# A four-stage attention and expert kernel: order of one step of the linear attention, a query scale moved, biases split early, fewer semaphore clears

## The chip, the cores and the metric

The kernel runs on one core of a Trainium2 chip. The metric is the device time of one execution in microseconds (us); three executions of the kernel before gave 4503.48, 4504.20 and 4504.74 us (median 4504.2). "TensorE" is the matrix engine (PE in the rows, PEld for its weight loads), "VectorE" is DVE, "ScalarE" is ACT, "GpSimd" is POOL, and "SyncE" is SP, which here only starts transfers.

## The reference, cut to what matters

Two layers are computed over 4096 tokens of width 256. Only the first part of the first layer is touched:

```
def _L0_attn_ref(X, Wq, Wv, q_norm_w, v_norm_w):
    K = X.reshape(B, L, H, d)                        # 16 heads of 16
    Q = rms_norm_multihead((X @ Wq.T).reshape(B, L, H, d), q_norm_w)
    V = rms_norm_multihead((X @ Wv.T).reshape(B, L, H, d), v_norm_w)
    W = jnp.cumsum(jnp.einsum('blhd,blhe->blhde', K, V), axis=1)
    return jnp.einsum('blhd,blhde->blhe', Q, W).reshape(B, L, D)
x = x + _L0_attn_ref(_layernorm(x), ...)
x = x + _L0_ffn_ref(_layernorm(x), ...)              # router: logits, top 2 of 16 experts
x = x + _L1_attn_ref(_layernorm(x), ...)
x = x + _L1_ffn_ref(_layernorm(x), ...)              # top 8 of 64 experts
```

## The kernel before

The program has seven stages, each a block of five instruction streams, one per engine, that meet only through semaphores: `linear_attention` (names la_), `experts` (ex_), `project` (pj_), `softmax_attention` (at_), `output_projection` (op_), `expert_pairs` (ep_) and `add_odd` (ao_). After each stage, `release` (L200 to L203) lets GpSimd clear the semaphores of the stage and then makes all engines wait for each other.

The first stage handles the tokens in 32 tiles of 128. It is a software pipeline: a loop over steps i from -12 to 41 is written out on every engine, and in step i an engine works on several tiles at once. Step i of TensorE (L794 to L842) is, in this order:

- `logits(i-8)`: the router's logits of a tile normalised earlier (L699). It first waits for `xa_ready`, VectorE's add of tile i-1 to x (L466). In one step of four (i = 12, 16, ...) `positions` (L711 to L716) follows, which needs the mask that VectorE's `choose` computes at the end of its previous step (L479 to L492).
- `queries(i+2)` and `keys(i+5)`: transposes (L723, L729). The keys need `xn`, which ScalarE writes (L602) after `roots` (L646), which needs VectorE's `squares_sum` (L448).
- `project(i+4)`: the query and value projection (L739).
- `outputs_T(i)`: state times queries (L749) and the masked scores times values (L757). It needs the state, a sum that GpSimd makes (L387) behind its two multiplications L369 and L376.
- `scores(i+1)` (L769), which VectorE then masks (`masked`, L440).
- `routed(i-7)` (L776), `outputs(i)` (L782), `update(i)` (L790).

VectorE's step is: router work of the group if there is any, `masked(i+1)`, `squares_sum(i+4)`, `update(i)` (the new key-value product times a block mask, L463, and the add to x, L466), statistics, `roots`, and in one step of four `choose` or `place`. Steps 27 and later have no keys left to transpose and steps 28 and later no projection; the logits run eight tiles behind and go on to step 39.

After the last `place`, GpSimd writes the routing table with indirect transfers (`scatter`, L396, two for a tile). The biases of the experts are loaded into buffers of the pipeline once these are free (L339 to L342), split into three bf16 parts by VectorE (L512 to L520, called in step NT+2 = 34), and stored to DRAM.

## Time and profile before

| | |
|---|---|
| median of three runs | 4504.2 us |
| the profiled execution's own time | 4506.27 us |
| its span | 4504.5 us |
| linear attention, from the start to the first instruction of the expert stage | 437.07 us |
| TensorE busy, whole span | 3984.1 us (88%) |

The span is divided by the semaphore barriers into stages, so a stage is read on its own: what it saves moves everything behind it forward. In a row of a timeline the first number is the start in us, the second the time from the first start to the last end, and `xN` how many instructions were merged; in brackets at the end stands how long the engine sat idle before and who ended it.

### The profile page before, as it was taken

How to read it: one execution, taken by the hardware profiler on the slowest of the kernel's cores; microseconds unless marked ns; L12 is line 12 of the kernel's file. 1: busy time of each engine (PE TensorE's matmuls, PEld its weight loads, DVE VectorE, ACT ScalarE, POOL GpSimd, SP SyncE). 2: the span in 40 equal slices, each digit the busy share in tenths (PEclk: the TensorE clock that was granted, in tenths of full speed). 3: DMA queues.
4: the chain of work that ended last, by engine and by line, in shares of the span. 5: the costliest groups of instructions: out<-in, count | busy, mean ns of one | idle time of the engine just before them, and what ended most of it. 6: DMA issues, size and time to landing. Idle time of an engine off the chain costs nothing. (4 is left out here: it accounts for less than half of the span.)

```text
span 4504.5 us, 54711 instructions
## 1 busy us (share of the span) xinstructions
PE 3984.1 (88%) x17866; PEld 3005.5 (67%) x17866; DVE 3574.9 (79%) x4436; ACT 2646.0 (59%) x3555; POOL 2209.0 (49%) x1837
## 2 busy tenths in 40 slices
PE   6774998683999999999999999999999999989563
PEld 3443554452788888888888888888888888867421
DVE  4454443774899999999999999999999999956611
ACT  4442333331677777777777777777777777742221
POOL 1234665464455555555555555555555555530154
PEclk8776999786999999999999999999999999989776
DMA  6001333666222232223222322232223223137296
GB/s 242 20 22 39 56 61 59 221 217 185 63 53 57 49 81 50 57 49 81 53 53 49 81 55 53 57 76 56 51 58 72 56 51 64 34 113 235 74 243 165
DMA packets 349678, 384.04 MB, mean 85 GB/s; under 512 B 141532, under 2 KB 279585, under 8 KB 336851
## 3 DMA queue, kind: packets, MB, share of 16 engines
q1 hardware_dynamic: 325334, 354.22, 30.8%
q0 software_dynamic: 24064, 26.32, 3.5%
q8 instruction: 147, 2.41, 0.2%
q14 instruction: 133, 1.09, 0.1%
HBM read 232.55 MB, written 117.84 MB: 78 GB/s over the span
## 5 line engine op out<-in xcount | busy, mean ns | idle before, releaser
L1523 POOL TENSOR_TENSOR at_pl<-at_pf,at_ph 128x512 fp32r<-128x512 f32 x1024 | 1330.0, 1299 | 1343.0 <-ACT at_ph L1670 1342.7
L1669 ACT ACTIVATE at_pf<-at_ps_s 128x1024 f32<-128x1024 f32 x1024 | 1051.0, 1026 | 747.5 <-PE at_ps_s L1719 747.5
L1586 DVE TENSOR_TENSOR at_pl<-at_pf,at_ph 128x512 fp32r<-128x512 f32 x1024 | 1355.4, 1324 | 20.6 <-ACT at_ph L1670 20.6
L1568 DVE TENSOR_REDUCE at_mx<-at_ps_u 128x2 f32<-128x1024 f32 x1024 | 1250.2, 1221 | 24.5 <-PE at_ps_u L1703 24.4
L1670 ACT ACTIVATE at_ph<-at_ps_s 128x1024 fp32r<-128x1024 f32 x1024 | 1042.7, 1018 | 0.0
L1719 PE MATMUL at_ps_s<-at_q,at_k 66*128 66x512 f32 x2048 | 820.7, 401 | 0.0
L1718 PE MATMUL at_ps_s<-at_q,at_k 128*128 128x512 f32 x2048 | 812.2, 397 | 0.3 <-ACT at_ph L1670 0.3
L1735 PE MATMUL at_ps_v<-at_ph,at_vh 128*128 128x512 f32 x2048 | 810.1, 396 | 0.2 <-POOL at_pl L1523 0.2
L1737 PE MATMUL at_ps_v<-at_pl,at_vh 128*128 128x512 f32 x2048 | 809.5, 395 | 0.0
L1736 PE MATMUL at_ps_v<-at_ph,at_vl 128*128 128x512 f32 x2048 | 809.2, 395 | 0.0
L1703 PE MATMUL at_ps_u<-at_k,at_qp 128*128 128x512 f32 x2048 | 648.0, 398 | 63.5 <-DMA at_q<-at_low 47.7
L1703 PEld LDWEIGHTS at_ps_u<-at_k,at_qp 128*128 128x128 f32 x2048 | 387.3, 190 | 163.6 <-issue 48.1
L1719 PEld LDWEIGHTS at_ps_s<-at_q,at_k 66*128 66x128 f32 x2048 | 387.6, 189 | 96.3
L1735 PEld LDWEIGHTS at_ps_v<-at_ph,at_vh 128*128 128x128 f32 x2048 | 389.3, 190 | 90.6 <-POOL at_pl L1523 0.6
L1736 PEld LDWEIGHTS at_ps_v<-at_ph,at_vl 128*128 128x128 f32 x2048 | 386.5, 189 | 94.6
L1737 PEld LDWEIGHTS at_ps_v<-at_pl,at_vh 128*128 128x128 f32 x2048 | 386.0, 188 | 89.9
L1718 PEld LDWEIGHTS at_ps_s<-at_q,at_k 128*128 128x128 f32 x2048 | 389.3, 190 | 84.3 <-ACT at_ph L1670 1.0
L440 DVE TENSOR_TENSOR la_at<-la_ps_a,C 128x512 f32<-128x512 f32 x128 | 79.5, 684 | 165.6 <-PE la_ps_a L769 165.6
L1191 DVE TENSOR_TENSOR pj_t<-pj_ps_e,pj_rope 128x1024 f32<-128x1024 f32 x128 | 149.7, 1216 | 62.4 <-PE pj_ps_e L1319 34.8
L1561 DVE TENSOR_TENSOR at_low<-at_raw,at_cut 128x512 fp32r<-128x512 f32 x128 | 170.0, 1328 | 18.0 <-DMA at_q<-at_low 17.9
L945 PE MATMUL ex_ps_g<-wgu,ex_xgT 128*128 x320 | 162.3, 630 | 0.0
L1661 ACT ACTIVATE at_qp<-at_q 128x512 fp32r<-128x512 f32 x128 | 143.5, 1123 | 29.6 <-DMA at_k<-kT 29.6
(254 smaller groups left out, 4116.1 us busy)
## 6 DMA issues: line engine op xcount, KB each, us to landing
at_k<-kT SPq DMA_DIRECT2D x64, 512.0 KB, 10.0
at_q<-qT SPq DMA_DIRECT2D x64, 512.0 KB, 9.3
wgu<-Wgu_in SPq DMA_DIRECT2D x64, 384.0 KB, 5.2
qT<-pj_rot SPq DMA_DIRECT2D x32, 512.0 KB, 3.1
vT<-pj_vo SPq DMA_DIRECT2D x32, 512.0 KB, 4.4
kT<-pj_rot SPq DMA_DIRECT2D x32, 512.0 KB, 3.1
at_raw<-qT SPq DMA_DIRECT2D x32, 512.0 KB, 4.7
at_raw<-kT SPq DMA_DIRECT2D x32, 512.0 KB, 6.6
```

Of the source, the lines that this page charges most:

```text
L1523: pool.tensor_tensor(pl[:, n % NP, at], pf[:, n % NP, at], ph[:, n % NP, at].bitcast(F32), ALU.subtract).then_inc(s["pl2_ready"], 1)
L1561: dve.tensor_tensor(low[:, i % 2], raw[hh][:, i * QB:(i + 1) * QB].bitcast(F32), cut[:, i % 2].bitcast(F32), ALU.subtract).then_inc(s["low ...
L1568: dve.tensor_reduce(mx[:, qb % 2, 2 * i:2 * i + 2], ps_u[:], X, ALU.max).then_inc(s["u_max"], 1)
L1586: dve.tensor_tensor(pl[:, n % NP, at], pf[:, n % NP, at], ph[:, n % NP, at].bitcast(F32), ALU.subtract)\
L1669: act.activation(pf[:, n % NP], ps_s[:, n % 2], ACT.Exp, scale=DH ** -0.5)
L1670: act.activation(ph[:, n % NP], ps_s[:, n % 2], ACT.Exp, scale=DH ** -0.5)\
L1703: m = pe.matmul(ps_u[:, w], tile, k1[hh][:, kb * QB:(kb + 1) * QB], start=True, stop=True)
L1718: pe.matmul(out, k1[hh][:, ks], q1[hh][:, qs], start=True, stop=False)
L1719: m = pe.matmul(out, k2[hh][0:MROW + 2, ks], q2[hh][0:MROW + 2, qs], start=False, stop=True)
L1735: pe.matmul(out, vh[:, hh, c], ph[:, n % NP, keys], start=c == 0, stop=False)
L1736: pe.matmul(out, vl[:, hh, c], ph[:, n % NP, keys], start=False, stop=False)
L1737: m = pe.matmul(out, vh[:, hh, c], pl[:, n % NP, keys], start=False, stop=c == KC - 1)
```

## The change

Six edits, all but the last in `linear_attention`.

1. TensorE's step begins with `queries`, `keys` and `project`; `logits` and `positions` stand between `outputs_T` and `scores`.
2. VectorE does `update(i)` ahead of `squares_sum(i+4)`.
3. The weight of the query norm is no longer applied by ScalarE to the queries (two ACTIVATEs with a scale) but by VectorE to the block mask (`blocksw`, once), by which the key-value product is multiplied. ScalarE copies the queries in one ACTIVATE.
4. The biases are loaded at the start, split in step -7 and stored then. ScalarE's first `squares` and VectorE's first `masked` wait for that.
5. The last four routed tiles alternate between two places in PSUM, with other waits.
6. The semaphores of three stages are cleared together after `project`, those of the other four at the end.

```
+            self.project()
+            self.release()
...
+            self.add_odd()
+            self.release()
...
-        def release():
-            nc.clear_and_free_semaphores(held)
-            nc.all_engine_barrier()
-        ctx.callback(release)
...
+                sp.dma_start(bsrc[:, 0:2 * F0], ins["bgu"]).then_inc(s["biases"], 16)
+                sp.dma_start(bsrc[:, 2 * F0:], ins["bd"]).then_inc(s["biases"], 16)
                 for q in range(1, Q):
                     load_x(q)
...
+                sp.wait_ge(s["bias_split"], 5)
+                sp.dma_start(self.bias_dram[:].rearrange("k e n -> e k n"), bpart).then_inc(s["bias_out"], 16)
...
-                        dve.tensor_tensor(dst, ps_k[:, 1], blocks.unsqueeze(1).broadcast_to([P, DC, P]), ALU.mult)\
+                        dve.tensor_tensor(dst, ps_k[:, 1], blocksw[:], ALU.mult)\
...
+                        link(dve.tensor_tensor(blocksw[:], blocks.unsqueeze(1).broadcast_to([P, DC, P]),
+                                               normw[:, :, 0:1].broadcast_to([P, DC, P]), ALU.mult))
+                    if i == -7:
+                        split_biases()
+                    if i == -1:
+                        dve.wait_ge(s["bias_out"], 16)
                     if tile(i + 1):
                         masked(i + 1)
+                    if tile(i):
+                        update(i)
                     if tile(i + 4):
                         squares_sum(i + 4)
                     if tile(i):
-                        update(i)
                         measure(i, (s["xa_ready"], i + 1), mv2, s["mv2_ready"])
...
-                    if i == NT + 2:
-                        split_biases()
...
-                        m = act.activation(qf[:, t % 3, c], src, ACT.Copy, scale=normw[:, c, 0:1])
-                    m.then_inc(s["q_ready"], 1)
+                    act.activation(qf[:, t % 3], ps_t[:, 1].rearrange("p (c l) -> p c l", c=DC), ACT.Copy).then_inc(s["q_ready"], 1)
...
-                    if tile(j):
-                        ...
-                        logits(j)
-                    if tile(j - 1) and (j - 1) % 4 == 3:
-                        ...
-                        positions((j - 1) // 4)
                     if tile(i + 2) or tile(i + 5):
...
                     if tile(i):
                         outputs_T(i)
+                    if tile(j):
+                        ...
+                        logits(j)
+                    if tile(j - 1) and (j - 1) % 4 == 3:
+                        ...
+                        positions((j - 1) // 4)
                     if tile(i + 1):
                         scores(i + 1)
```

TensorE in step 16, where positions come, before (la_wg is the router's weight, la_mask the mask of `choose`, la_qn and la_xn the normalised queries and tokens):

```order
L699 MATMUL la_ps_o<-la_wg,la_xrT 128x16 [waits la_xrT_ready,la_lg_ready,la_xa_ready]
L699 MATMUL la_ps_o<-la_wg,la_xrT 128x16
L711 MATMUL la_ps_o<-la_mask,tri 128x64 [waits la_mask_ready,la_seen_ready,la_lg_ready,la_xa_ready]
L713 MATMUL la_ps_o<-la_mask,ones_bf 128x48
L713 MATMUL la_ps_o<-la_mask,ones_bf 128x32
L713 MATMUL la_ps_o<-la_mask,ones_bf 128x16
L716 MATMUL la_ps_o<-la_seen,ones_bf 128x64
L723 MATMUL la_ps_t<-C,la_qn 128x128 [waits la_q_ready,la_qn_ready,la_xnT_ready,la_xrT_ready]
L723 MATMUL la_ps_t<-C,la_qn 128x128
L729 MATMUL la_ps_t<-C,la_xn 128x128 [waits la_xn_ready]
L729 MATMUL la_ps_t<-C,la_xn 128x128
L739 MATMUL la_ps_qv<-la_wqv,la_xnT 128x512 [waits la_qc_ready,la_xnT_ready]
```

and in the changed kernel the same step (its line numbers are larger by 10):

```order
L733 MATMUL la_ps_t<-C,la_qn 128x128 [waits la_q_ready,la_qn_ready,la_xnT_ready,la_xrT_ready]
L733 MATMUL la_ps_t<-C,la_qn 128x128
L739 MATMUL la_ps_t<-C,la_xn 128x128 [waits la_xn_ready]
L739 MATMUL la_ps_t<-C,la_xn 128x128
L749 MATMUL la_ps_qv<-la_wqv,la_xnT 128x512 [waits la_qc_ready,la_xnT_ready]
L749 MATMUL la_ps_qv<-la_wqv,la_xnT 128x512
L767 MATMUL la_ps_k<-la_at,la_vn 32x128 [waits la_vn_ready,la_at_ready,la_kvm_ready]
L767 MATMUL la_ps_k<-la_at,la_vn 32x128 x15
L709 MATMUL la_ps_o<-la_wg,la_xrT 128x16 [waits la_xrT_ready,la_lg_ready,la_xa_ready]
L709 MATMUL la_ps_o<-la_wg,la_xrT 128x16
L721 MATMUL la_ps_o<-la_mask,tri 128x64 [waits la_mask_ready,la_seen_ready,la_lg_ready,la_xa_ready]
```

The two waits on VectorE (`xa_ready` and `mask_ready`) no longer stand ahead of the transposes and the projection; the only wait on the way to these is now `xn_ready`.

VectorE late in the stage, step 34, before (16x768 are the biases, la_lg the logits of the seventh group):

```order
L433 SCALAR_TENSOR_TENSOR la_nb<-la_mv,la_rstd 128x4 [waits la_rstd2_ready]
L516 CAST la_at<-la_xnT 16x768 [waits la_oT_ready,la_biases]
L517 TENSOR_TENSOR la_sq<-la_xnT,la_at 16x768 [waits la_bias_split]
L518 CAST la_at<-la_sq 16x768 [waits la_bias_split]
L519 TENSOR_TENSOR la_xnT<-la_sq,la_at 16x768 [waits la_bias_split]
L520 CAST la_at<-la_xnT 16x768 [waits la_bias_split]
L472 TENSOR_TENSOR la_lg<-la_ps_o,la_bg 128x64 [waits la_l_ready,la_bias_split]
```

and VectorE at the start of the changed kernel, behind the statistics of the first tiles:

```order
L537 TENSOR_TENSOR la_pq<-C,la_normw 128x4 [waits la_norms]
L539 TENSOR_TENSOR la_blocksw<-C,la_normw 128x256
L430 BN_STATS la_stats<-x_sb 128x6 [waits la_mv1_ready,la_x1,la_own]
L431 BN_AGGR la_mv<-la_stats 128x2 [waits la_own]
L520 CAST la_at<-la_at 16x768 [waits la_biases]
L521 TENSOR_TENSOR la_sq<-la_at 16x768 [waits la_bias_split]
L522 CAST la_at<-la_sq 16x768 [waits la_bias_split]
L523 TENSOR_TENSOR la_at<-la_sq,la_at 16x768 [waits la_bias_split]
L524 CAST la_at<-la_at 16x768 [waits la_bias_split]
```

The five operations have left the place ahead of the logits of the seventh group and stand some 380 us earlier, between the statistics of the fifth and the sixth tile.

## Rows read from the trace of the kernel before

**Rows 1.** Stretches of the first stage: us, PE, PEld, DVE, ACT, POOL busy (instructions), clock, DMA share, GB/s
```profile
44.36:114.39 70.03, 49.44 (x464) 31.49 (x464) 36.42 (x90) 32.10 (x95) 12.48 (x20) 0.85 0.51 187
114.39:342.68 228.29, 163.22 (x1382) 110.05 (x1382) 113.76 (x334) 102.88 (x294) 62.38 (x83) 0.78 0.08 24
342.68:378.48 35.80, 23.29 (x272) 17.83 (x273) 20.71 (x63) 12.76 (x39) 13.20 (x16) 0.86 0.10 31
378.48:437.07 58.59, 16.52 (x115) 12.50 (x114) 28.43 (x111) 8.04 (x20) 30.52 (x29) 0.58 0.13 30
```

**Rows 2.** Who waited for whom, 44 to 380 us: total us, times, longest
```profile
DVE la_at L440 <- PE la_ps_a L769: 161.2, 31, 7.2
PE la_ps_o L699 <- DVE x_sb L466: 62.3, 23, 2.9
PE la_ps_t L729 <- ACT la_xn L602: 20.6, 7, 2.9
```

**Rows 3.** Timeline of a step without logits (63.24 to 73.46 us)
```profile
63.24 2.48 DVE L440 TENSOR_TENSOR la_at<-la_ps_a,C 128x512 f32<-128x512 f32 x4 [4.77 <-PE la_ps_a L769]
...
65.64 0.68 DVE L448 TENSOR_REDUCE la_ss<-la_sq 128x32 f32<-128x512 f32 x1
66.23 0.41 DVE L463 TENSOR_TENSOR la_kvm<-la_ps_k,C 128x256 f32<-128x256 f32 x1
...
66.56 0.42 DVE L466 TENSOR_TENSOR x_sb<-la_ps_o,x_sb 128x256 f32<-128x256 f32 x1
66.58 0.58 ACT L602 ACTIVATE la_xn<-x_sb,la_nb,la_rstd 128x256 f32<-128x256 f32 x1
...
67.22 0.69 PE L729 MATMUL la_ps_t<-C,la_xn 128*128 128x128 f32 x2 [2.94 <-ACT la_xn L602]
```

**Rows 4.** Timeline of a step with logits (126.80 to 137.65 us)
```profile
126.80 2.48 DVE L440 TENSOR_TENSOR la_at<-la_ps_a,C 128x512 f32<-128x512 f32 x4 [7.24 <-PE la_ps_a L769]
...
130.60 0.62 PE L699 MATMUL la_ps_o<-la_wg,la_xrT 128*128 128x16 f32 x4 [2.75 <-DVE x_sb L466]
...
131.53 3.35 PE L739 MATMUL la_ps_qv<-la_wqv,la_xnT 128*128 128x512 f32 x4
...
136.49 1.17 PE L769 MATMUL la_ps_a<-la_qz,la_xnT 32*128 32x256 f32 x16
```

**Rows 5.** The same windows view inside two steps, 121.6 to 128.4 us
```profile
121.60:125.00 3.40, 3.40 (x23) 2.05 (x24) 0.00 (x0) 1.61 (x5) 0.00 (x0) 0.50 0.02 5
125.00:128.40 3.40, 2.84 (x49) 2.12 (x40) 1.60 (x3) 1.01 (x3) 0.00 (x0) 1.00 0.00 0
```

**Rows 6.** Timeline of a step with positions (257.32 to 271.64 us)
```profile
264.99 0.21 PE L711 MATMUL la_ps_o<-la_mask,tri 128*128 128x64 bf16 x1 [3.17 <-DVE la_mask L492]
```

**Rows 7.** Timeline, GpSimd's state sum in step 27 (began at 342.68)
```profile
348.59 0.72 POOL L387 TENSOR_TENSOR la_state<-la_state,la_kvm 128x256 f32<-128x256 f32 x1
```

**Rows 8.** Timeline of the bias split, 394 to 402 us
```profile
394.10 1.01 PE L699 MATMUL la_ps_o<-la_wg,la_xrT 128*128 128x16 f32 x4 [0.56 <-ACT la_xrT L664]
...
397.84 0.55 DVE L516 CAST la_at<-la_xnT 16x768 bf16<-16x768 f32 x1 [7.30 <-DMA la_xnT<-bd_in]
398.42 0.95 DVE L517 TENSOR_TENSOR la_sq<-la_xnT,la_at 16x768 f32<-16x768 f32 x1
...
401.54 0.23 DVE L472 TENSOR_TENSOR la_lg<-la_ps_o,la_bg 128x64 f32<-128x64 f32 x1
```

**Rows 9.** Timeline of GpSimd alone, 398 to 408 us
```profile
398.82 1.41 POOL L396 DMA_INDIRECT table<-la_entry,la_slot  x1 [0.31 <-issue]
400.54 1.25 POOL L396 DMA_INDIRECT table<-la_entry,la_slot  x1 [0.30 <-issue]
406.65 0.98 POOL L396 DMA_INDIRECT table<-la_entry,la_slot  x1 [4.86 <-DVE la_entry L508]
```

**Rows 10.** GpSimd's release between stages, all seven: ns min/median/max, first and last start
```profile
L202 POOLq EVENT_SEMAPHORE_RANGE_CLEAR  x7: 67/240/418, 436.3 to 4504.1; - x7
```

**Rows 11.** Timeline of ScalarE at the start, 10 to 20 us
```profile
16.42 0.60 ACT L631 ACTIVATE la_sq<-la_ps_qv 128x512 f32<-128x512 f32 x1 [2.53 <-PE la_ps_qv L739]
```

More of the change, by code:

```diff
@@ L143, in __init__ @@
         self.nc, self.ins, self.out = nc, ins, out
-        self.sems = 0
+        self.held = []
     def build(self):
@@ L193, in scope, with release @@
         ps = lambda name, shape, dt=F32: ctx.enter_context(nc.psum_tensor(f"{stage}_{name}", shape, dt))
-        held = []
         def sem(name):
-            held.append(nc.alloc_semaphore(f"{stage}_{name}"))
-            return held[-1]
-        def release():
-            nc.clear_and_free_semaphores(held)
-            nc.all_engine_barrier()
-        ctx.callback(release)
+            self.held.append(nc.alloc_semaphore(f"{stage}_{name}"))
+            return self.held[-1]
         return ctx, sb, ps, sem
+    def release(self):
+        self.nc.clear_and_free_semaphores(self.held)
+        self.nc.all_engine_barrier()
+        self.held = []
     def linear_attention(self):
@@ L220, in linear_attention @@
             pq = sb("pq", [P, DC, 2])
+            blocksw = sb("blocksw", [P, DC, P])
             stats = sb("stats", [P, 2, 2, 6])
@@ L279, in linear_attention @@
             BW = 2 * F0 + D
-            bsrc, brest = (buf[0:E].rearrange("p a b -> p (a b)")[:, 0:BW] for buf in (xnT, sq))
-            bpart = at[0:E].rearrange("p h l -> p (h l)")[:, 0:3 * BW // 2].bitcast(BF16).rearrange("p (k n) -> p k n", k=3)
+            room = at[0:E].rearrange("p h l -> p (h l)")
+            bsrc, brest = room[:, 0:BW], sq[0:E].rearrange("p a b -> p (a b)")[:, 0:BW]
+            bpart = room[:, BW:BW + 3 * BW // 2].bitcast(BF16).rearrange("p (k n) -> p k n", k=3)
             below, begin = (buf.rearrange(f"p {a} -> p ({a})")[:, 0:(ST0 + 1) * E].rearrange("p (n e) -> p n e", e=E)
@@ L298, in sums, with routed_at @@
                 return (TB - 2) * (t // TB) + max(0, min(t % TB, LAST) - 1)
+            def routed_at(t):
+                return ps_qv[:, 0:D] if t >= NT - 4 and t % 2 else ps_t[:, 0]
             vn3 = vn[:].rearrange("p r g t d -> p r (g t d)")
@@ L663, in routed_T @@
                         act.wait_ge(s["l_ready"], t - 1)
[L664 removed]
+                    act.activation(xrT[:, t % 2], routed_at(t), ACT.Copy).then_inc(s["xrT_ready"], 1)
                 for i in range(FIRST, END):
@@ L823, in _ @@
                         outputs_T(i)
+                    if tile(j):
+                        if i > 0:
+                            pe.wait_ge(s["xa_ready"], min(i, NT))
+                        if j >= 4 and j % 4 == 0:
+                            pe.wait_ge(s["lg_ready"], j // 4)
+                        if j >= 5 and j % 4 == 1:
+                            pe.wait_ge(s["pos_read"], j // 4)
+                        logits(j)
+                    if tile(j - 1) and (j - 1) % 4 == 3:
+                        pe.wait_ge(s["xa_ready"], min(i, NT))
+                        pe.wait_ge(s["lg_ready"], (j - 1) // 4 + 1)
+                        positions((j - 1) // 4)
                     if tile(i + 1):
@@ L830, in _ @@
                             pe.wait_ge(s["q_ready"], i + 3)
-                        if tile(i - 8):
+                        if i - 7 >= NT - 2:
+                            pe.wait_ge(s["xrT_ready"], i - 8)
+                        elif 0 < i - 7 <= NT - 4:
                             pe.wait_ge(s["xrT_ready"], i - 7)
+                        if i - 7 == NT - 3:
+                            pe.wait_ge(s["qc_ready"], NT)
                         routed(i - 7)
```

20 lines of the change are left out of this document (3 added, 17 removed).

## Prediction

> **What bounds the kernel now.** I read the table of stages first: all but two small edits stand in linear attention, which ends at 437.07 us of 4504.5 and hands its end to the next stage through a barrier, so a microsecond saved there is one off the total. Second, the windows of that stage [rows 1]: no engine is busy throughout. From 44.36 to 342.68 us TensorE works 71% of the time at a mean granted clock of 0.85 and 0.78, VectorE 50%. Third, who waited for whom [rows 2]: VectorE's `masked` waits for TensorE's scores 31 times (161.2 us), and TensorE waits for VectorE's add to x 23 times (62.3 us, 2.7 each), in the steps without logits for `xn` instead (7 times, 20.6 us). So a step is a loop of two engines that take turns: TensorE's scores, `masked`, VectorE's chain, TensorE again. Fourth, one step of each kind. Let M be the start of `masked`. Without logits [rows 3] the tokens' statistics are at M+2.40, the key-value product at +2.99, the add at +3.33, `xn` at +3.34 and the keys at +3.98; the next M follows 6.24 us later, a step of 10.22. With logits [rows 4] these wait for the add and start at M+3.80, and the step is 10.85. Steps with positions wait once more, 3.17 us for the mask, and take 14.32 [rows 6].
>
> **The clock.** Inside a step there are stretches of some 3.4 us with the granted clock at 0.50, which is the 1.2 GHz level, and others at 1.00, the 2.4 GHz level [rows 5]; the projection runs at the lower one (3.35 us) [rows 4]. Such a stretch, in which TensorE is always busy, costs half its length, 1.70 us. The step of 10.85 had one, so it would be 9.15 without; the step of 10.22 would be 8.52. Steps 8 to 26 take 228.29 us [rows 1]; four have positions, and at 14.32 each they leave 171.0 for the other fifteen, 11.40 each. That is 2.25 above 9.15: one such stretch in every step and a second in a third of them.
>
> **The change, part by part.** All against the profiled execution, whose own time is 4506.27 us (span 4504.5 and 1.8 around it), 2.1 above the median.
>
> *Order in VectorE's step.* The product and the add now stand ahead of `squares_sum`. Their starts are 0.33 apart and the add lasts 0.42, of which some 0.07 lies beside the next operation, so `squares_sum` starts 0.68 later [rows 3]. `roots`, `xn` and the keys hang on it and come at M+4.66. In the steps with logits the add was the gate before and is no longer.
>
> *Steps 1 to 7* (70.03 us [rows 1]) have no logits; the transposes led TensorE's step already. They only lose: 0.68 each is 4.8. A longer wait before the keys may also bring a second slow stretch; in one step of five, 0.34 each, I take +1.0 a step, **+7.0**. Bounds: 0, should the later `squares_sum` be absorbed by an earlier add and statistics, and +17, if every step gets a second stretch (7 x 2.4).
>
> *Steps 8 to 26.* The new loop is: keys at M+4.66, then the 6.24 less 1.70 of a warm step without logits, 4.54, and the logits in line behind `outputs_T`, 0.62 [rows 3, 4]. That is 9.82 warm, 0.67 more than 9.15. What it gives back is the mask: positions now stand late in the step, where the mask (3.17 us behind the logits' place) has long been there, so the four steps pay only for the matmuls, about 0.4 each. The clock decides the rest. I take one slow stretch in each step and a second in one of ten, 1.87 us, since one idle stretch of TensorE per step remains and the second one, behind the logits in positions' steps, goes: 11.69 a step. 19 x 11.69 + 4 x 0.4 - 0.9 (step 16 begins a new state and has no product to wait for) = 222.8 against 228.29, **-5.5**. Bounds: with 1.70 it is 219.6, -8.7; with today's 2.25 it is 230.0, +1.7. Without the position steps there would be no gain: each of the other fifteen goes from 11.40 to 11.69.
>
> *Steps 27 to 30* (35.80 us [rows 1]). No keys are left. In step 27 the state, GpSimd's sum, is complete at M+6.63 [rows 7], and `outputs_T` can't start before it; work that stood ahead of it during that wait, the logits, now stands behind it. I take 0.62 a step, **+2.4**, bounds -1 (step 28 no longer waits for its mask) and +5 (the lower clock after the wait doubles what follows).
>
> *The biases at the end.* VectorE sat idle 7.30 us for the bias transfer and then spent 397.84 to 401.54 on five operations, while the seventh group's logits were ready at 394.10 + 1.01 = 395.11 [rows 8]. The group is ready some 6.4 us earlier. But GpSimd's scatters follow, and these are a queue: GpSimd was idle for VectorE only 4.86 us at 406.65, where 0.31 is its usual gap, so 4.55 is gained. Two scatters that lay beside the split's subtraction of 0.95 took 1.41 and 1.25 us, where the next takes 0.98 [rows 8, 9]; they should shrink by 0.43 and 0.27 as well: **-5.2**, bounds -4.55 and -6.4. [...]
>
> *The releases.* GpSimd's clear is at 436.3 and the next stage's first instruction at 437.07, 0.8 us, and there are seven [rows 1, 10]. Five go, 3.9; the semaphores that they cleared are cleared in the two that stay, about 5 x 0.24 = 1.2: **-2.7**, bounds -2.6 and -4.0.
>
> *The start.* The split now needs two transfers of 16 rows and its five operations (3.9 us as in [rows 8]) ahead of ScalarE's first `squares`. This starts at 16.42 us, after 2.53 us of waiting for the projection [rows 11], and VectorE's own work there waits for transfers of x as well; so I take **0**. If the biases land late or x by as much behind them, the whole start shifts: bound +3. The store of the split biases is waited for before tile 0's `masked`, some 20 us after the split: 0.
>
> *No term.* ScalarE copies the queries in one operation instead of two, beside a VectorE that is waited for: 0, bounds -1 and +1. The block mask product reads a tensor of the same size (0.41 us [rows 3]), one extra operation is in the start: 0. The last four routed tiles in two places: a buffer wait less at the end, 0, bound -1.
>
> Sum: 7.0 - 5.5 + 2.4 - 5.2 - 2.7 = -4.0. From 4504.2 this gives **4500.2 us**. About 9 us, 0.2%, is what a measurement of this kernel can tell from no change.
>
> **Rivals.**
>
> *A: the clock comes back.* If TensorE, opening the step with its longest piece of work and no longer stopped by the add and the mask, is granted the higher level for more of it, the mean penalty of steps 8 to 26 falls from 1.87 to, say, 1.0: 19 x 0.87 = 16.5 less, **4484**. For it: the clock is 0.86 in steps 27 to 30, where steps are short, against 0.78 [rows 1], so steps without a slow stretch exist. Against: steps 1 to 7 have this very order on TensorE, with a wait of 2.94 us for `xn` in each and a clock of only 0.85.
>
> *B: slower, by the second stretch.* The keys come 0.68 later than now in steps without logits and 0.14 later in the others, and the logits are added to the part behind them. If each step of 8 to 26 then has two slow stretches, it takes 9.82 + 3.4 less what the stretch shares with idle time, 12.7: 19 x 1.0 more, **4519**. The point from which it decides: a mean penalty above 2.16 eats the whole gain of these steps, above 2.9 the kernel is slower by 9. For it: the penalty is 2.25 now. Against: today's second stretches come with the additional stop for the mask or the add, which is gone.
>
> *C: it does not do what it says.* The mask may still be late, because `choose` also starts later, behind an update and statistics that now wait for outputs_T: then 4 x 2.5 us come back, **4510**. Against: positions moves by more than 5 us (from the step's head to behind `outputs_T`) and the wait was 3.17 [rows 6].
>
> *D: the start is bound by the biases*, +3, **4503**: inside "no change".
>
> **Chances.** Forecast with D 0.47; A 0.30, C 0.08, B 0.15. Faster by over 0.2% (under 4495.2): A and a part of the forecast's own spread (its terms at the good ends give -8.7 instead of -5.5 and +4.8 for +7.0), 0.35. Slower by over 0.2% (over 4513.2): B, 0.14. Within: 0.51. The likeliest case alone has 4492 to 4510; the range with A and most of B is 4483 to 4514.
>
> **What would show it.** Right: `masked` to keys 4.66 in every step; no wait of logits for the add or of positions for the mask; steps 1 to 7 together 75 to 79 us, steps 8 to 26 about 223 us at a clock near 0.8; the seventh group's logits on VectorE at 395 in place of 401.5 and no idle 4.86 on GpSimd; two releases. Wrong: keys at M+4.0 still in steps 1 to 7, steps 8 to 26 under 210 or over 235 us, a first `masked` later than before, or a wait in the tail that takes the place of the split.

## The result: slower by 0.2 to 0.3%, where "no change" was forecast

The changed kernel took 4516.68 us (median of 9 runs, 4512.07 to 4522.57) beside 4503.48 of the kernel before (9 runs): ratio 1.003, 95% interval 1.002 to 1.004, so 13 us slower and just above the range of 4483 to 4514. The same kernel, run once more beside the experiments, took 4508.04 us (11 runs) beside 4500.68: ratio 1.0017 (1.0008 to 1.0026), 7.4 us slower. Both say slower, the second by a time inside the range; the forecast was 4 us faster.

The profiled execution has a span of 4510.0 us, 5.5 more than before. The windows of its first stage, in the same stretches as [rows 1] (steps 1 to 7, 8 to 26, 27 to 30, and from the last `masked` to the expert stage), columns as there:

```profile
42.11:121.39 79.28, 54.05 (x464) 34.05 (x464) 35.77 (x91) 30.58 (x88) 12.49 (x20) 0.81 0.47 170
121.39:346.75 225.36, 161.01 (x1381) 105.76 (x1382) 112.50 (x333) 98.05 (x275) 62.39 (x83) 0.80 0.08 25
346.75:388.67 41.92, 29.61 (x273) 22.30 (x273) 20.62 (x64) 11.71 (x36) 13.19 (x16) 0.71 0.08 26
388.67:452.18 63.51, 19.29 (x115) 14.65 (x114) 24.86 (x106) 8.05 (x20) 29.63 (x30) 0.53 0.11 26
```

Beside [rows 1] the stretches changed by +9.25, -2.93, +6.12 and +4.92 us. TensorE has the same number of matmuls in each (to within one), VectorE too, but for the five operations of the bias split that left the tail, and the granted clock (third number from the end) fell in all but the second. Linear attention ends at 452.18 in place of 437.07 us. The second profile of the same kernel gives the first three stretches again (79.48, 225.39, 41.92), but another tail:

```profile
391.61:445.17 53.56, 18.63 (x115) 14.15 (x114) 25.09 (x106) 8.16 (x20) 29.58 (x29) 0.53 0.14 31
```

That is 5.0 us less than the 58.59 of before, where the first profile had 4.9 more. The two tails are told apart below.

Who waited for whom in the changed kernel, 42 to 380 us (total us, times, longest):

```profile
DVE la_at L445 <- PE la_ps_a L779: 127.2, 30, 7.7
...
PE la_ps_t L739 <- ACT la_xn L611: 89.0, 26, 3.6
```

TensorE's 23 waits for the add (62.3 us in [rows 2]) are gone, and so are its four for the mask, 12.0 us in the same view of before. In their place it waits 26 times for `xn`, 3.4 us each, where [rows 2] has 7 waits of 2.9. Here is the step that corresponds to [rows 3], a timeline of the changed kernel (start, length, engine, in brackets the idle time before and who ended it):

```profile
64.04 2.48 DVE L445 TENSOR_TENSOR la_at<-la_ps_a,C 128x512 f32<-128x512 f32 x4 [5.59 <-PE la_ps_a L779]
...
66.44 0.41 DVE L468 TENSOR_TENSOR la_kvm<-la_ps_k,la_blocksw 128x256 f32<-128x256 f32 x1
...
67.10 0.68 DVE L453 TENSOR_REDUCE la_ss<-la_sq 128x32 f32<-128x512 f32 x1
...
68.68 0.69 PE L739 MATMUL la_ps_t<-C,la_xn 128*128 128x128 f32 x2 [3.60 <-ACT la_xn L611]
...
69.16 3.62 PE L749 MATMUL la_ps_qv<-la_wqv,la_xnT 128*128 128x512 f32 x4
...
72.58 1.06 PE L759 MATMUL la_ps_k<-la_qf,la_state 128*128 128x128 f32 x4
```

`squares_sum` is 0.66 us later behind `masked` (3.06 instead of 2.40), and the keys come at M+4.64 (3.98 before, 4.66 forecast). Behind them everything runs at the lower level: the projection 3.62 us, and now `outputs_T` as well, 1.06. This step took 12.19 us; it was 10.22. It is one of the slow ones: of the steps 2 to 7, four took 10.9 to 11.0 us, the old step plus the gate, and two took 12.2, with a second slow stretch. Step 1 took 11.0 us where it had 8.7.

Steps 28 to 30 at the end of the loop, TensorE alone:

```profile
365.18 1.19 PE L759 MATMUL la_ps_k<-la_qf,la_state 128*128 128x128 f32 x4 [4.32 <-POOL la_state L392]
...
373.79 0.68 PE L759 MATMUL la_ps_k<-la_qf,la_state 128*128 128x128 f32 x4 [2.48 <-POOL la_state L392]
...
382.60 1.20 PE L759 MATMUL la_ps_k<-la_qf,la_state 128*128 128x128 f32 x4 [1.86 <-POOL la_state L392]
383.73 1.94 PE L767 MATMUL la_ps_k<-la_at,la_vn 128*32 128x128 f32 x32
385.59 1.04 PE L709 MATMUL la_ps_o<-la_wg,la_xrT 128*128 128x16 f32 x4
386.56 2.11 PE L779 MATMUL la_ps_a<-la_qz,la_xnT 32*128 32x256 f32 x16
```

`outputs_T` waits for GpSimd's sum, as forecast, and the logits stand behind it; but in step 30 all that follows runs at the lower level (scores 2.11 us, 1.17 in [rows 4]), and in step 29 the logits and the scores do (1.04 and 2.11). These two steps took 8.8 and 9.8 us instead of 6.6 each.

### The profile page after: what moved, and what is told of

Same layout as the page of the kernel before. It is cut to its first block and busy times, and to the rows that moved or that the text cites. A ratio compares the mean times of both kernels' runs of the same rounds, so it can differ in the third digit from the quotient of the medians.

```text
span 4510.0 us, 54615 instructions
## 1 busy us (share of the span) xinstructions
PE 3992.0 (89%) x17866; PEld 3006.6 (67%) x17866; DVE 3573.9 (79%) x4437; ACT 2639.5 (59%) x3523; POOL 2209.8 (49%) x1837
## 5 line engine op out<-in xcount | busy, mean ns | idle before, releaser
L1582 DVE TENSOR_REDUCE at_mx<-at_ps_u 128x2 f32<-128x1024 f32 x1024 | 1250.4, 1221 | 24.2 <-PE at_ps_u L1717 23.9
L445 DVE TENSOR_TENSOR la_at<-la_ps_a,C 128x512 f32<-128x512 f32 x128 | 79.5, 684 | 136.0 <-PE la_ps_a L779 136.0
```

The lines of the kernel that those rows point to most:

```text
L1582: dve.tensor_reduce(mx[:, qb % 2, 2 * i:2 * i + 2], ps_u[:], X, ALU.max).then_inc(s["u_max"], 1)
```

## Two different tails

In the first profile, TensorE and ScalarE at the end of the stage:

```profile
414.31 0.67 PE L786 MATMUL la_ps_t<-C,la_xr 128*128 128x128 f32 x2
...
419.52 0.38 ACT L674 ACTIVATE la_xrT<-la_ps_t 128x256 f32<-128x256 f32 x1 [5.72 <-remote]
...
420.90 0.67 PE L786 MATMUL la_ps_qv<-C,la_xr 128*128 128x128 f32 x2
...
426.59 0.38 ACT L674 ACTIVATE la_xrT<-la_ps_qv 128x256 f32<-128x256 f32 x1 [6.20 <-remote]
```

ScalarE's copy waits for two transposes that by the record end at 414.98, and it starts at 419.52; the next starts 5.0 us after its transposes' recorded end. The view names no instruction that released it, only "remote", and the ends of matmuls are modelled in a profile. So by the record TensorE's answer came 4.5 and 5.0 us late (and once more, by 2.6, at 398). In the second profile no such wait occurs: there the copy starts 0.03 us after the transposes' recorded end,

```profile
414.54 0.67 PE L786 MATMUL la_ps_t<-C,la_xr 128*128 128x128 f32 x2
...
415.24 0.38 ACT L674 ACTIVATE la_xrT<-la_ps_t 128x256 f32<-128x256 f32 x1 [1.21 <-PE la_ps_t L786]
```

and the tail is 9.95 us shorter. The forecast for the tail, -5.2, is what the second profile (-5.0) shows.

## The experiments

All times are medians. The ratio, with its 95% interval, is to the kernel before run beside each; it is estimated from all runs and can differ from the ratio of the medians by some 0.0006. Those medians of the kernel before were 4500.01, 4500.68, 4501.13 and 4503.19 us, so kernels of different groups are compared by what they differ from it. "Steps" are the stretches of [rows 1] in the kernel's own profile.

| kernel | us | ratio | steps 1-7 | 8-26 | 27-30 | tail |
|---|---|---|---|---|---|---|
| before (profile) | 4500 to 4503 | 1 | 70.0 | 228.3 | 35.8 | 58.6 |
| changed, first profile | 4516.68 | 1.003 (1.002-1.004) | 79.3 | 225.4 | 41.9 | 63.5 |
| order_both | 4516.58 | 1.0043 (1.003-1.0057) | 79.4 | 225.4 | 41.9 | 59.0 |
| vector_order_only | 4501.86 | 1.0009 (1.0-1.0018) | 79.5 | 223.0 | 35.0 | 57.1 |
| tensor_order_only | 4486.80 | 0.9973 (0.9964-0.9982) | 71.9 | 208.7 | 38.9 | 57.3 |
| all_but_orders | 4495.06 | 0.9992 (0.9983-1.0001) | 69.9 | 228.3 | 35.8 | 53.4 |
| changed_again | 4508.04 | 1.0017 (1.0008-1.0026) | 79.5 | 225.4 | 41.9 | 53.6 |
| releases_only | 4498.31 | 0.9997 (0.9988-1.0006) | 72.3 | 225.8 | 35.8 | 56.4 |
| biases_only | 4495.98 | 0.9991 (0.9982-1.0) | 70.0 | 228.3 | 35.8 | 52.8 |
| changed_vector_back | 4483.59 | 0.9958 (0.9944-0.9972) | 70.0 | 208.9 | 38.8 | 53.2 |
| sum_between | 4494.46 | 0.9982 (0.9973-0.9991) | 75.4 | 213.3 | 38.8 | 52.8 |
| logits_between | 4490.77 | 0.9983 (0.997-0.9996) | 72.2 | 213.0 | 38.0 | 54.6 |
| logits_and_sum_between | 4499.81 | 1.0002 (0.9993-1.0011) | 75.6 | 223.6 | 37.9 | 51.8 |
| scale_only | 4501.74 | 1.0003 (0.9994-1.0012) | 70.0 | 228.3 | 35.8 | 57.3 |
| fill_changed | 4474.95 | 0.9936 (0.9922-0.995) | 72.5 | 194.6 | 37.9 | 63.6 |
| fill_vector_back | 4463.96 | 0.9915 (0.9901-0.9929) | 66.1 | 192.7 | 37.4 | 63.2 |
| fill_half | 4471.21 | 0.9929 (0.9916-0.9943) | 72.3 | 194.5 | 39.2 | 63.7 |
| fill_before | 4478.53 | 0.9941 (0.9928-0.9955) | 66.0 | 205.2 | 35.4 | 60.2 |

The second table is what the account rests on. It has the time in which the granted clock stood at 0.50, the lower level, summed over windows of 0.1 us through the loop of each profile, in us. In brackets is the same in the prediction's unit, its slow stretches of 3.4 us.

| slow time | steps 1-7 | 8-26 | 27-30 |
|---|---|---|---|
| before | 20.5 (6) | 99.0 (29) | 10.2 (3) |
| changed, both profiles, and order_both | 30.7 (9) | 92.2 (27) | 24.0 (7) |
| vector_order_only | 30.7 (9) | 92.2 (27) | 10.2 (3) |
| tensor_order_only | 23.9 (7) | 68.3 (20) | 13.7 (4) |
| changed_vector_back | 20.5 (6) | 68.3 (20) | 13.7 (4) |
| sum_between | 27.3 (8) | 68.3 (20) | 13.7 (4) |
| fill_changed | 13.7 (4) | 6.8 (2) | 10.2 (3) |
| fill_vector_back | 0 | 0 | 10.2 (3) |
| fill_before | 0 | 13.7 (4) | 3.4 (1) |

### The parts alone

**Both orders** (edits 1 and 2 on the kernel before; the words behind `#` are not in the code):

```
-                    if tile(j): ... logits(j)            # head of TensorE's step
-                    if tile(j - 1) ...: ... positions((j - 1) // 4)
                     if tile(i): outputs_T(i)
+                    if tile(j): ... logits(j)
+                    if tile(j - 1) ...: ... positions((j - 1) // 4)
                     if tile(i + 1): scores(i + 1)
...
-                    if tile(i + 4): squares_sum(i + 4)   # VectorE
                     if tile(i): update(i)
+                    if tile(i + 4): squares_sum(i + 4)
```

> The kernel before with the two changes of order alone (logits and positions behind outputs_T on TensorE; update ahead of squares_sum on VectorE). Theory 1, the order of the steps is what made the change slower: steps 1 to 7 take about 79 us (70.0 before), steps 8 to 26 about 225, steps 27 to 30 about 43, so linear attention is 14 us longer than before and the kernel is at about 4518 us. Theory 2, the loss is in the tail (three late signals of TensorE, some 12 us together, that came with the biases' or the buffers' change): the stage is longer by 2 us at most and the kernel within 4 us of before. Theory 3, both: 4508 to 4513.

Measured 1.0043, 16.6 us slower, and the steps 79.4, 225.4, 41.9: theory 1, the loss is in the orders. Theory 2 falls.

**Only VectorE's order** (the last three lines of that diff):

> The kernel before with update ahead of squares_sum on VectorE, nothing else. Theory 1: keys move from 3.98 to 4.66 us behind the start of masked; steps 1 to 7 get the whole loss (79 us instead of 70), steps 8 to 26 stay at 228 since there the add, not the statistics, is waited for, and the kernel is 8 to 10 us slower than before. Theory 2: the 0.68 us cost 5 us in steps 1 to 7 at most, and the kernel is less than 5 us slower.

Steps 1 to 7 have the whole loss, as expected, but steps 8 to 26 gained 5.3 us: with the logits still at the head of the step, what TensorE waits for there is the add, and that now comes earlier (23 waits of 2.2 us in place of 2.7). Windows of this kernel:

```profile
45.38:124.86 79.48, 54.25 (x464) 34.27 (x464) 35.77 (x91) 32.23 (x95) 12.49 (x20) 0.81 0.43 160
124.86:347.83 222.97, 162.08 (x1381) 105.74 (x1382) 111.98 (x333) 102.58 (x294) 62.39 (x83) 0.79 0.08 25
```

Sum: 1.0009, 1.9 us slower. Theory 1 had the loss in the steps 1 to 7 and missed the total (8 to 10); theory 2 had the total (under 5) and missed the loss. The gain that sets them apart was in neither.

**Only TensorE's order** (the first part of the diff):

> The kernel before with logits and positions behind outputs_T on TensorE, nothing else. Theory 1: steps 1 to 7 stay at 70 us; steps 8 to 26 are shorter than in the changed kernel by the 0.68 us of the gate, about 225 - 13 = 212; steps 27 to 30 get the +8 us; sum about 8 us faster than before. Theory 2: with the gate earlier each step has the same number of slow clock stretches and steps 8 to 26 stay at 225; the kernel is 3 to 6 us slower than before.

Theory 1 holds, and more: 13.2 us faster. Steps 8 to 26 are 19.6 us shorter, and the clock is 0.84. The last stretch grew by 3.1 us, where theory 1 had 8:

```profile
45.60:117.54 71.94, 51.36 (x463) 32.56 (x464) 36.42 (x91) 32.27 (x95) 12.47 (x20) 0.83 0.47 176
117.54:326.25 208.71, 155.35 (x1381) 102.28 (x1382) 114.24 (x333) 102.19 (x294) 62.34 (x83) 0.84 0.08 27
```

The four steps with positions are 12.3 of these 19.6 us: they took 56.9 us together and take 44.6 without the wait for the mask. The other fifteen are 0.5 us shorter each.

The two orders are not additive: 0.9973 x 1.0009 = 0.9982 stands against 1.0043, some 27 us. Where the transposes of the keys start, in us behind the start of `masked`, shows why. In steps 1 to 7 it is 3.98 before and with edit 1, 4.64 with edit 2. In steps 8 to 26 it is 4.5 to 5.1 before (8.2 to 8.4 with positions), 4.64 with edit 2 alone (8.1 to 8.2 with positions), 3.98 with edit 1 alone, and 4.64 with both. So in steps 8 to 26 edit 2 costs nothing while the add gates the keys, and costs 0.66 a step as soon as edit 1 has taken that gate away. The slow time follows: 20 stretches with edit 1, 27 with both.

**All but the orders** (edits 3 to 6 on the kernel before):

> Edits 3 to 6 without the two orders: query scale on VectorE, biases at the start, two places for the last routed tiles, two releases. Theory 1: start 2 us earlier, tail 5 us shorter, releases 2.7 us: about 9 us faster than before, 4494 us, and no late signals in the tail. Theory 2 (the late signals come with these edits): the tail is 3 us longer than before as in the changed kernel, and the kernel is the same as before or slower.

0.9992; the tail is 5.2 us shorter (53.37), the steps are untouched, and no late answers in the tail. The start (first `masked` at 34.56) was not earlier: that of the first profile (32.24) is scatter, the profiles have 32.2 to 36.8. The gain in the median was 5 us rather than 9, with an interval (0.9983 to 1.0001) that just holds no change.

**The changed kernel again:**

> The changed kernel as it is, a second profile. Theory 1, the three late signals of TensorE in the tail (2.6, 4.5 and 5.0 us) belong to this program: they come again at the same places, the tail from the last masked to the expert stage is 63 us and the time 4513 to 4517. Theory 2, they were an accident of one execution: the tail is 53 to 54 us (5.2 less than in the kernel with the two orders alone, 59.0), the span some 10 us under 4510, and the time 4507 to 4511.

4508.04 and the tail 53.56: theory 2, in the time, in the tail and nearly in the span (4503.2, 6.8 under 4510). As the fill kernels below have late answers in all four profiles, "an accident of one execution" is too strong: they come and go, and what decides is open. They don't explain the first comparison's higher time either: its profiled execution, the one seen to have them, took 4512.07 us and was the fastest of the nine.

**Releases only:**

```
             self.project()
+            self.release()
...
             self.add_odd()
+            self.release()
...
-        ctx.callback(release)
```

> The kernel before with two releases in place of seven, nothing else. Theory 1, what stood in the prediction: 2.7 us faster. Theory 2: stages overlap now, each starts before the last one's semaphores are cleared, and the gain is larger, 6 us or more. Theory 3: one clear of many semaphores, and other semaphore numbers, cost what the barriers gave: no difference.

2.4 us faster in the median, with an interval (0.9988 to 1.0006) that holds theories 1 and 3. More can be had from the profiles: from the first instruction of the expert stage to the end there are 4062.9 us on average in the seven that have seven releases (4059.6 to 4067.4) and 4060.3 in the eleven that have two (4055.2 to 4064.4), 2.6 less. With this scatter the 2.6 is itself uncertain by about 3 (twice the error of the two means, an estimate from the 18 values), so that it agrees with the forecast's 2.7 is in part luck. The kernel before's profile, 4067.4, is the longest, so the 9.6 us that the two main profiles differ by behind linear attention are mostly scatter. This kernel's steps 1 to 7 took 72.3 us and 8 to 26 225.8, against 70.0 and 228.3, though no instruction of the loop is changed: 7 and 28 slow stretches in place of 6 and 29. Differences of this size in one stretch of a single profile mean little.

**Biases only:**

```
                 sp.dma_start(normw[:], ins["qvw"]).then_inc(s["norms"], 16)
+                sp.dma_start(bsrc[:, 0:2 * F0], ins["bgu"]).then_inc(s["biases"], 16)
+                sp.dma_start(bsrc[:, 2 * F0:], ins["bd"]).then_inc(s["biases"], 16)
...
+                    if i == -7:
+                        split_biases()
...
-                    if i == NT + 2:
-                        split_biases()
```

> The kernel before with the biases loaded and split at the start, nothing else. Theory 1: tail 5.2 us shorter (53.4 in place of 58.6), masked of tile 0 where it was (34.5 to 36): 5 us faster. Theory 2: the transfers ahead of those of x delay the start by up to 3 us, and 2 us are left.

Theory 1: tail 52.77, 5.8 us shorter, first `masked` at 34.06, and 4.7 us faster in the median (0.9982 to 1.0).

**Scale only:**

```
-                        dve.tensor_tensor(dst, ps_k[:, 1], blocks.unsqueeze(1).broadcast_to([P, DC, P]), ALU.mult)
+                        dve.tensor_tensor(dst, ps_k[:, 1], blocksw[:], ALU.mult)
...
-                        m = act.activation(qf[:, t % 3, c], src, ACT.Copy, scale=normw[:, c, 0:1])
+                    act.activation(qf[:, t % 3], ps_t[:, 1].rearrange("p (c l) -> p c l", c=DC), ACT.Copy)
```

> The kernel before with the query norm's weight in the block mask (edit 3) and nothing else. Theory 1, what stood in the prediction: within 1 us of before, since ScalarE's copy of the queries is off the path. Theory 2: the queries' copy, 0.4 us shorter, lets the outputs' scaled copy and the roots come sooner and takes 0.1 to 0.2 us from each step: 3 to 6 us faster.

Theory 1: 1.0003 (0.9994 to 1.0012), and every stretch of the loop as before to 0.02 us.

### How much the keys' gate is worth

**The changed kernel with VectorE's order back** (`squares_sum` first, all else changed):

```
+                    if tile(i + 4): squares_sum(i + 4)
                     if tile(i): update(i)
-                    if tile(i + 4): squares_sum(i + 4)
```

> The changed kernel with squares_sum ahead of update again on VectorE. Theory 1, the order on VectorE is what costs, together with the new order on TensorE: steps 1 to 7 take 72 us (79.3 in the changed kernel), steps 8 to 26 209 (225.4), steps 27 to 30 39 (41.9), so it is 27 us faster than the changed kernel, and with the tail and the releases some 20 us faster than before, 4480 us: the best version. Theory 2, the late signals stay in the tail: 10 us of that are lost, 4490 us.

Theory 1 to within 4 us: 4483.59, which is 17 us faster than before and 24 faster than the changed kernel run beside it.

```profile
46.66:116.62 69.96, 49.38 (x464) 31.47 (x464) 36.42 (x91) 30.53 (x88) 12.48 (x20) 0.85 0.50 185
116.62:325.49 208.87, 155.34 (x1382) 102.26 (x1382) 114.26 (x334) 97.88 (x275) 62.38 (x83) 0.84 0.08 27
325.49:364.27 38.78, 25.35 (x272) 19.40 (x273) 20.81 (x63) 11.79 (x36) 13.17 (x16) 0.82 0.09 28
```

Edit 2 alone costs 9.5, 16.5 and 3.1 us in these stretches. Its gate of 0.68 us would be 4.8 and 12.9 in the first two; the rest goes with the clock (0.81 for 0.85, 0.80 for 0.84, 0.71 for 0.82), that is with 3, 7 and 3 slow stretches more. In steps 27 to 30, which have no keys, the clock is all of it: the last two take 7.1 us each here, the 6.6 of before and the logits, and 8.8 and 9.8 in the changed kernel.

**Half of the gate** (the product, then `squares_sum`, then the add to x):

```
                     if tile(i): update(i)        # now the product alone
                     if tile(i + 4): squares_sum(i + 4)
+                    if tile(i): add(i)
```

> The changed kernel with VectorE's update in two parts: product, then squares_sum, then the add to x. The keys' gate is then 4.3 us behind masked, between 3.98 (squares_sum first) and 4.66 (changed). Theory 1, what costs is the gate of the keys, in each step, and the slow clock that a longer wait brings: steps 1 to 7 take about 75 us and steps 8 to 26 about 217, half way between 70/209 (squares_sum first) and 79/225 (changed), so 12 us faster than the changed kernel. Theory 2, the number of slow stretches jumps at some length of wait: either nothing of the loss is left (70/209) or all of it (79/225).

The keys start at 4.31. Theory 1: 75.4 us in steps 1 to 7 (75 expected), 213.3 in 8 to 26 (217), between the ends, some 14 us faster than the changed kernel. But the slow time in steps 8 to 26 is that of changed_vector_back (20 stretches), as theory 2 would have it; what is left of the loss there, 4.5 us, is less than the bare 0.33 x 19 = 6.3.

**Logits between projection and `outputs_T`**, with `squares_sum` first:

```
+                    if tile(j): ... logits(j)
                     if tile(i): outputs_T(i)
-                    if tile(j): ... logits(j)
                     if tile(j - 1) ...: ... positions((j - 1) // 4)
```

> The changed kernel with squares_sum first on VectorE and the logits between project and outputs_T on TensorE (positions stay behind outputs_T). Theory 1: outputs_T waits for the state until 6.6 us behind masked in steps whose projection ends by then, and the logits (0.5 us) fill this gap: steps 8 to 26 take 0.3 to 0.5 us less each, 200 to 204 us in place of 208.9, and steps 27 to 30 lose less: 6 to 10 us faster than the version with logits behind outputs_T (4483.6). Theory 2: TensorE runs the whole way from the keys to the scores without a pause in nearly all steps, so the place of the logits is without effect: within 2 us.

Neither: it is some 7 us slower than with the logits behind, outside both theories, though its runs spread widely (4480 to 4510) and the two intervals touch. Single steps take 9.6 us, but others 13.6 to 13.8, and the clock of steps 8 to 26 is 0.80 (25 slow stretches for 20):

```profile
119.38:332.38 213.00, 160.47 (x1381) 107.64 (x1382) 114.21 (x334) 97.77 (x275) 62.43 (x83) 0.80 0.08 26
```

**The same with the sum between:**

> Both: product, squares_sum, add on VectorE, and logits between project and outputs_T on TensorE. The state is complete 0.6 us sooner than with squares_sum first, and the keys come 0.3 us later. Theory 1 (the gate of the keys decides): 5 to 12 us slower than logits_between. Theory 2 (the state decides): as fast or faster.

9 us slower than logits_between by the medians: theory 1, the gate of the keys, in its range, with intervals that just touch.

### Is it the clock?

Up to here the clock was only read beside the times. The next four kernels keep every order and add transposes of the identity in TensorE's wait, which nobody reads. The keys start at 4.64 in fill_changed and at 3.98 in fill_vector_back and fill_half, as without filling:

```
                         if tile(i + 1):
                             pe.wait_ge(s["q_ready"], i + 2)
+                        if tile(i) and tile(i + 2):
+                            for _ in range(12):
+                                pe.transpose(ps_t[:, 1, 0:P], ident, ident)
                         if tile(i + 2):
                             m = queries(i + 2)
```

> The changed kernel with 12 transposes of the identity at the head of TensorE's step (steps 0 to 29), in the wait for the tokens; nobody reads their results. Theory 1, the slow clock behind the wait costs: the granted clock of steps 8 to 26 rises from 0.80 to over 0.95 and a step comes down from 11.9 to about 9.9 us (the warm step of the prediction, 9.82): steps 8 to 26 take about 190 us, steps 1 to 7 about 66, the kernel is some 45 us faster than the changed one. Theory 2, the slow clock has nothing to do with the wait: clock 0.80 as before, and 12 transposes (2.5 to 4 us in a wait of about 3.5) cost nothing or up to 0.5 us a step, up to 15 us slower.

> The same 12 transposes in the version with squares_sum first on VectorE (changed_vector_back, 208.9 us for steps 8 to 26, clock 0.84). Theory 1: clock over 0.95, steps 8 to 26 about 19 x 9.2 = 175 us plus what the transposes reach over the gate (0 to 0.3 us a step); the difference to fill_changed is the bare gate, 0.68 x 26 = 18 us or less, instead of the 24 to 27 us without the filling. The fastest version of all, about 4450. Theory 2: no faster than 4483.6, rather up to 15 us slower.

In fill_half there are six, and in the kernel before the twelve stand ahead of the logits, behind the same waits:

> Six transposes in place of 12, otherwise as fill_vector_back. Theory 1: they fill 1.2 us of a wait of about 3: part of the effect, clock between 0.84 and 0.95, or none. Theory 2: no effect, as they hide in the wait.

> The kernel before with the same 12 transposes ahead of the logits, in TensorE's wait for the add (2.7 us). Theory 1: the clock of steps 8 to 26 rises from 0.78 to over 0.9, the step to 9.2 us and 12 us in the ones with positions, 185 us in place of 228: 35 to 45 us faster than before. Theory 2: nothing, or up to 1 us a step slower, as the transposes last longer than the wait.

All four are 25 to 39 us faster than the kernel before run beside them, with more work for TensorE. Windows of steps 8 to 26 in fill_changed:

```profile
114.65:309.29 194.64, 156.49 (x1609) 114.67 (x1608) 112.50 (x334) 96.67 (x275) 62.38 (x83) 0.98 0.09 29
```

of steps 1 to 7, 8 to 26 and the tail in fill_vector_back:

```profile
43.45:109.51 66.06, 50.79 (x547) 35.96 (x548) 36.42 (x90) 30.58 (x88) 12.51 (x20) 1.00 0.57 202
109.51:302.22 192.71, 157.69 (x1608) 114.73 (x1608) 114.28 (x333) 97.06 (x275) 62.40 (x83) 1.00 0.09 29
...
339.59:402.75 63.16, 18.04 (x115) 13.38 (x114) 24.87 (x106) 8.36 (x21) 29.61 (x29) 0.54 0.11 26
```

and of steps 8 to 26 in fill_before:

```profile
110.48:315.71 205.23, 159.90 (x1608) 115.05 (x1608) 113.76 (x334) 100.00 (x293) 62.37 (x83) 0.97 0.09 27
```

The clock of steps 8 to 26 is 0.97 to 1.00 in all four, and these steps are 14 to 31 us shorter. Theory 1's direction holds in all. Six transposes do nearly what twelve do in steps 8 to 26 (194.5 and 192.7, with a clock of 0.98 where at most 0.95 was expected), but nothing in steps 1 to 7 (72.3 and 66.1, and 70.0 without any). The difference between the two orders on VectorE is 11 us here, 24 without filling. In steps 8 to 26, where neither is slow any more, it is 1.9 us of 16.5: at the higher level edit 2 costs next to nothing there (the keys are later, but the state is ready at 6.65 us behind `masked` in place of 6.78), and nearly all that it costs in the changed kernel goes with the clock.

The size was overestimated each time. fill_changed is some 36 us faster than the changed kernel, 45 were expected, and a step took 10.2 us, 9.9 expected. fill_vector_back has 10.1 a step for 9.2 and 4464 us for 4450. fill_before is 24.7 us faster than before for 35 to 45, as its steps with positions stayed at 14.1 us, where 12 were expected. TensorE in a step of fill_vector_back shows the main reason:

```profile
130.61 1.50 PE L814 MATMUL la_ps_t<-C 128*128 128x128 f32 x12
131.95 0.38 PE L732 MATMUL la_ps_t<-C,la_qn 128*128 128x128 f32 x2
133.71 0.44 PE L738 MATMUL la_ps_t<-C,la_xn 128*128 128x128 f32 x2 [1.38 <-ACT la_xn L610]
133.99 1.88 PE L748 MATMUL la_ps_qv<-la_wqv,la_xnT 128*128 128x512 f32 x4
136.51 0.68 PE L758 MATMUL la_ps_k<-la_qf,la_state 128*128 128x128 f32 x4 [0.64 <-POOL la_state L392]
```

The projection takes 1.88 us and not 3.35 to 3.62, and then `outputs_T` waits for GpSimd's state. At the full clock the state is the next bound, so a slow stretch is not worth its 1.70 us but what lies above that bound: a step without logits comes down from 10.2 to 9.6, not to the 8.52 of the prediction, and in steps 8 to 26 the 20 slow stretches that went were worth 16.2 us, 0.8 each. The tails of these four kernels are 60.2 to 63.7 us. In fill_before, whose bias split is still there, that is 1.6 us more than before, with one late answer. In fill_vector_back ScalarE waits as in the first profile, and this eats some 10 us of the gain (63.2 for 53.2 in changed_vector_back):

```profile
370.32 0.38 ACT L673 ACTIVATE la_xrT<-la_ps_t 128x256 f32<-128x256 f32 x1 [4.91 <-remote]
...
376.73 0.38 ACT L673 ACTIVATE la_xrT<-la_ps_qv 128x256 f32<-128x256 f32 x1 [5.54 <-remote]
```

fill_vector_back, 4463.96 us, beats both kernels: the changed one with `squares_sum` first and TensorE kept at work.

## Why the prediction was wrong, by its own steps

| term | forecast | first profile | second profile |
|---|---|---|---|
| start, to the second `masked` | 0 | -2.3 | +0.5 |
| steps 1 to 7 | +7.0 | +9.3 | +9.5 |
| steps 8 to 26 | -5.5 | -2.9 | -2.9 |
| steps 27 to 30 | +2.4 | +6.1 | +6.1 |
| tail | -5.2 | +4.9 | -5.0 |
| five releases | -2.7 | (-9.6) | (-9.4) |

The numbers in brackets are all of the span behind linear attention; in the comparison of 18 profiles the releases' part is -2.6. With that, the second profile's terms sum to +5.6 us, and 7.4 was measured (3.6 to 11.7); the first comparison, 13.2, has more, and its profiled execution has the late answers, 10 us. Whether the other eight executions had them isn't shown, and that the profiled one was the fastest of the nine leaves the higher time of the first comparison open.

- **What bounds the kernel.** Right: two engines in turn, with the gate of the keys in steps 1 to 7. The gate at M+4.66 was 4.64, and `outputs_T` in steps 27 and 28 began 6.65 us behind M, where 6.63 was read for step 27. The waits for the add and for the mask went, so rival C (4 x 2.5 us come back) didn't happen. Rival D neither. Nearly all its signs of being right came (79.3 us for 75 to 79, 225.4 for about 223, the clock 0.80, no waits), and the kernel was slower all the same: the signs were too wide for a sum of 4 us.
- **The step that failed is the number of slow stretches.** Three terms of the loop were each too favourable, by 2.5, 2.6 and 3.7 us, 8.8 together, and no term had the wrong sign. The forecast let one step of five get a second stretch in steps 1 to 7, so 7.4 in place of 6; nine came. In steps 8 to 26 it had one per step and a second in one of ten, so 21, "since one idle stretch of TensorE per step remains"; 27 came, 29 were there before. In steps 27 to 30 it had no term for the clock, only the bound of +5; four more came. The stretch of idle time that remains became longer, 3.6 us in place of 2.9 and 3.4 on average, and that was left out: with edit 1 but without edit 2, 20 stretches came in steps 8 to 26, the forecast's own number.
- **Where the forecast was luckier than it looks.** 27 stretches at its price of 1.70 would be 10 us more than 21, and it was off by 2.6. The price was too high as well (225.4 us less the warm loop's 187.3 is 38, that is 1.4 for each of the 27), and the two errors cancel in part. The price was read from a window as wide as the stretch [rows 5]; that slow time had begun at 118.2 us and lasted 6.8.
- **Rival B** (a slower kernel by the second stretch) is the nearest to what happened: its mechanism, later keys and logits in line, at a mean penalty near 2.0 us a step (11.86 measured less the warm 9.82) and not yet 2.16. It was priced in steps 8 to 26 alone. It decided the sign together with steps 1 to 7 and 27 to 30, where the change has nothing to give back. Its "above 2.9 the kernel is slower by 9" is a slip: by its own sum that point is 2.55, and 2.9 would be 15 us.
- **Rival A** (the clock comes back) didn't happen, not even for edit 1 by itself, though the clock rose from 0.78 to 0.84 there. Rival A has a mean penalty of 1.0 us. The forecast's own 1.87, with the gate of 0.68 left out, gives 19 x 11.01 + 0.7 = 209.9 us for steps 8 to 26, and tensor_order_only has 208.7. So the forecast had all it needed to see that edit 1 alone is the better change. It charged edit 2 with its gate and never asked what edit 1 would be without it; the 24.5 us between changed_again and changed_vector_back are the price of that one exchange of two lines.
- **The price of a slow stretch**, 1.70 us, was read from the windows and holds as an upper bound. The filled kernels show that 0.6 us of it is real in a step without logits, 0.8 in steps 8 to 26 with `squares_sum` first, since the state's sum is next.
- **The tail** was right as a term (-5.0, -5.2 in all_but_orders, -5.8 in biases_only). With the split gone, the scatters in the place of the two that took 1.41 and 1.25 us take 0.98 each in all_but_orders and biases_only, as the term had it. Late answers of TensorE were nowhere in the prediction; nothing in the profile of before speaks of them.
- **Scale and routed places**: nothing, as taken, for the scale; the places weren't tried alone. **Releases**: -2.6 against -2.7, but uncertain by as much.

## What to carry to other kernels

Where two engines take turns, move nothing between the operation that opens the turn and the one that the idle engine waits for, even if the total work is the same: here 0.68 us of VectorE in front of `squares_sum` cost 24 us, and 11 once TensorE's wait was filled. Measure each exchange of order alone and both together, for the two here gave +2, -13 and together +17 us. And where TensorE idles in every step, look at the granted clock behind the wait, and count the slow time and not only the waits: work that nobody reads was worth more here (25 us on the kernel before) than any order tried (17).

## What the runs showed of the hardware

- Filling a wait of about 3 us per step with 12 transposes of 1.5 us together raised the granted clock of steps 8 to 26 from 0.84 to 1.00, and made the kernel some 20 us faster (4463.96 against 4483.59; 22 when each is taken beside its own runs of the kernel before). In the kernel before it went from 0.78 to 0.97, and the kernel was 24.7 us faster. Six transposes gave 0.98 in the same steps and 0.83 in steps 1 to 7, where twelve gave 1.00.
- In the loop of the kernel before the clock stands at 0.50 for 130 us of 334; with TensorE's wait 0.66 us longer in every step (changed_vector_back to the changed kernel) it is 147 us in place of 103.
- The same program gave the same length of a stretch to 0.3 us in two executions (79.28 and 79.48, 225.36 and 225.39), and another program with the same loop gave 72.3 and 225.8 for 70.0 and 228.3: where slow stretches fall repeated here, yet isn't determined by the order of the loop's instructions alone.
- TensorE's results came 2.6 to 5.0 us after the recorded end of its matmuls in the tail of the first profile of the changed kernel, and 2.6 to 4.4 us after it in the tails of fill_before and fill_vector_back, not in the second profile. The cause is open. That they go with more activity of TensorE before is a guess that the two profiles of the changed kernel speak against, since they have the same loop.
- An indirect transfer issued by GpSimd took 1.41 and 1.25 us beside VectorE's subtractions of 16x768, and 0.98 in the same place without them.
